# 32x32 transposes on VectorE in place of TensorE's turns of attention's output, and the first expert's mask made by ScalarE

## The reference

```python
# attention, no softmax over keys: the softmax runs over the 8 features of a head
scores = einsum('bhqk,bhsk->bhqs', qh, kh) / sqrt(8)
out = softmax(einsum('bhqs,bhsk->bhqk', scores, vh), axis=-1)
x = x + heads_side_by_side(out) @ wo_w.T + wo_b
# experts, on the normalised x (t), e = each of the two best experts
h1 = t @ w1.T + 2 * (t @ a1[e].T) @ b1[e].T
h3 = t @ w3.T + 2 * (t @ a3[e].T) @ b3[e].T
act = silu(h1) * h3
out_e = act @ w2.T + 2 * (act @ a2[e].T) @ b2[e].T
x = x + sum over e of weight[e] * out_e
```

## Time and profile before

| | |
|---|---|
| median of 3 runs | 298.84 us (298.49 to 299.08) |
| span of the profiled execution, first to last instruction | 296.7 us |
| time around the span (median less span) | 2.1 us |
| busy: PE, PEld, DVE, ACT, POOL | 287.4, 238.4, 221.4, 187.5, 187.0 us |
| mean granted TensorE clock | 0.992 |

### The profile page before, as it was taken

The page is one execution under the profiler, slowest core; times in us unless marked ns, Lnnn a source line. Parts: engine busy times, 40 slices in busy tenths (PEclk is TensorE's granted clock), DMA queues, the critical chain, the costliest instruction groups (busy, mean ns, idle before and its releaser), DMA issues. The chain is left out here.

```text
span 296.7 us, 4518 instructions
## 1 busy us (share of the span) xinstructions
PE 287.4 (97%) x1487; PEld 238.4 (80%) x1487; DVE 221.4 (75%) x607; ACT 187.5 (63%) x310; POOL 187.0 (63%) x186
## 2 busy tenths in 40 slices
PE   8779999999999999999999999999999999999995
PEld 6557888878888888888888888888888887878874
DVE  3878986995689658894589765895579965795295
ACT  1467967674945966757755868459656658655532
POOL 3375599288970889419990589608982389518930
PEclk9979999999999999999999999999999999999999
DMA  5720020200220021200211011200012000200002
GB/s 147 287 66 9 0 73 1 72 1 11 97 73 0 0 72 38 71 1 2 71 50 60 0 49 59 71 0 2 1 37 73 0 0 35 75 1 0 0 2 71
DMA packets 7225, 12.45 MB, mean 42 GB/s; under 512 B 1825, under 2 KB 3234, under 8 KB 7202
## 3 DMA queue, kind: packets, MB, share of 16 engines
q1 hardware_dynamic: 6768, 11.77, 12.0%
q10 hardware_dynamic: 434, 0.39, 0.4%
HBM read 10.03 MB, written 2.13 MB: 41 GB/s over the span
## 5 line engine op out<-in xcount | busy, mean ns | idle before, releaser
L989 ACT ACTIVATE silu<-h_ps 128x512 f32<-128x512 f32 x64 | 37.4, 596 | 31.4 <-PE h_ps L641 29.8
L1639 POOL TENSOR_TENSOR um_lo<-umf,um_hi 128x1024 fp32r<-128x1024 f32 x7 | 16.9, 2414 | 60.5 <-ACT um_hi L981 60.5
L641 PE MATMUL h_ps<-um_hi,b_hi 128*128 128x512 f32 x128 | 51.4, 401 | 0.0
L641 PE MATMUL h_ps<-um_lo,b_hi 128*128 128x512 f32 x128 | 50.3, 393 | 0.5 <-DVE um_lo L1309 0.5
L641 PE MATMUL h_ps<-um_hi,b_lo 128*128 128x512 f32 x128 | 49.9, 390 | 0.0
L1322 DVE TENSOR_TENSOR act_first<-silu,h_ps 128x512 f32<-128x512 f32 x32 | 21.4, 680 | 20.9 <-ACT silu L989 16.1
L1322 DVE TENSOR_TENSOR act_second<-silu,h_ps 128x512 f32<-128x512 f32 x32 | 21.7, 679 | 16.6 <-PE h_ps L641 14.7
L1661 POOL TENSOR_TENSOR scaled<-act_second,ratio 128x512 f32<-128x512 f32 x24 | 31.5, 1313 | 1.3 <-DVE act_second L1322 1.3
L641 PEld LDWEIGHTS h_ps<-um_lo,b_hi 128*128 128x128 f32 x128 | 24.0, 188 | 6.9 <-DVE um_lo L1309 1.4
L981 ACT CAST um_hi<-umf 128x1024 fp32r<-128x1024 f32 x14 | 14.8, 1055 | 23.2 <-DVE umf L1303 22.2
L641 PEld LDWEIGHTS h_ps<-um_hi,b_lo 128*128 128x128 f32 x128 | 24.1, 188 | 4.5
(11 more groups left out here) (278 smaller groups left out, 789.2 us busy)
## 6 DMA issues: line engine op xcount, KB each, us to landing
chosen<-choice_dram SPq DMA_DIRECT2D x7, 512.0 KB, 3.6
x_in<-in_x_dram SPq DMA_DIRECT2D x7, 256.0 KB, 2.9
ctx_in<-in_ctx_t_dram SPq DMA_DIRECT2D x7, 256.0 KB, 3.2
out_dram<-y SPq DMA_DIRECT2D x7, 256.0 KB, 2.0
act_second<-in_hidden_w_dram SPq DMA_DIRECT2D x1, 512.0 KB, 4.1
act_second<-in_lora_w_dram SPq DMA_DIRECT2D x1, 512.0 KB, 5.6
v_parts<-in_down_w_dram SPq DMA_DIRECT2D x1, 512.0 KB, 5.3
ctx_in<-in_ctx_t_dram ACTq DMA_DIRECT2D x2, 128.0 KB, 3.2
```

What stands on the lines that cost most here:

```text
L641: mm = nc.tensor.matmul((h1_ps, h3_ps)[s][n % 2][:], b13[w][:, s, c * P:(c + 1) * P], um[k][m][:, s, :], start=False, stop=(i == 2), skip_ ...
L989: nc.scalar.activation(silu[:, n % SILU_RING, :], h1_ps[n % 2][:], ACT.Silu).then_inc(silu_done.sem, 1)
L1639: nc.gpsimd.tensor_tensor(um[1][1][:], umf[1][:], as_f32(um[1][0][:]), ALU.subtract)\
```

## The change

From the third block on (`n >= AHEAD`, AHEAD = 2) the attention product gets its operands in reverse, so that `b_ps` holds features x tokens. `turn_o` on VectorE transposes each 32x32 square of it in place into `heads` (SBUF): a partition then holds tokens of one 32-group, and its columns the features of one group of four heads, so the softmax's groups of 8 lie side by side in the columns as before. Maximum and shift read `heads`. After GpSimd's division a second 32x32 transpose on VectorE, `turn_heads`, writes `heads_t`, which the projection reads; TensorE's turn and ScalarE's copy of it go for these blocks. The bank `b_ps` is free for the down products after `turn_o`.

For every block but the first the first expert's mask is made by ScalarE: |row's expert - chosen expert| (Abs) into `distance`, then Relu(1 - distance). It stands behind `z_high(b, 2)`, ahead of `ctx_high`, which `z_high(b, 2)` has passed. VectorE makes the second mask after `mask_u(0)`.

```diff
             def attention_out(n, i=WHOLE):
...
-                by_tile(o_bank(n, i), lambda t: q_t[:, t * P:(t + 1) * P], lambda t: ktv[:, t, :], i=i)\
-                    .then_inc(o_mm.sem, 1)
+                queries, pairs = (lambda t: q_t[:, t * P:(t + 1) * P]), (lambda t: ktv[:, t, :])
+                if n < AHEAD:
+                    by_tile(o_bank(n, i), queries, pairs, i=i).then_inc(o_mm.sem, 1)
+                else:
+                    by_tile(o_bank(n, i), pairs, queries, i=i).then_inc(o_mm.sem, 1)
...
             def project(n, i=WHOLE):
...
+                elif n >= AHEAD:
+                    pe.wait_ge(logits_done.sem, logits_done.of(n - 1))
...
-                        used = (ktv_done, o_shifted)[k]
-                        pe.wait_ge(used.sem, used.of(b + 2))
+                        if k == 0:
+                            pe.wait_ge(ktv_done.sem, ktv_done.of(b + 2))
+                        else:
+                            pe.wait_ge(o_turned, b + 3 - AHEAD)
...
                 hidden(b, 0)
                 hidden(b, 1)
-                turn_heads(b + 1)
...
+            def first_mask(n):
+                if n == 1:
+                    sc.wait_ge(row_expert_in, 16)
+                sc.wait_ge(chosen_in.sem, chosen_in.of(n))
+                nc.scalar.activation(tile4(distance), chosen_index(0), ACT.Abs, bias=row_expert_sb[:, 0:1], scale=-1.0)\
+                    .then_inc(expert_gap.sem, 1)
+                sc.wait_ge(expert_gap.sem, expert_gap.of(n))
+                if n > 1:
+                    sc.wait_ge(v_part_done.sem, v_part_done.of(n - 2))
+                    sc.wait_ge(umf_done.sem, umf_done.of(n - 2))
+                nc.scalar.activation(masks[n % 2][:, 0, :], distance[:], ACT.Relu, bias=1.0, scale=-1.0)\
+                    .then_inc(first_mask_done.sem, 1)
...
             exp_o(2)
             exp_ratio(1)
+            first_mask(1)
             ctx_high(3)
...
-                heads_turned(b + 1)
...
                 z_high(b, 1)
+                z_high(b, 2)
+                first_mask(b + 1)
                 if b + 3 < BLOCKS:
                     ctx_high(b + 3)
-                z_high(b, 2)
                 um_high(b + 1, 0)
...
+            def turn_o(n):
+                ve.wait_ge(o_mm.sem, o_mm.of(n))
...
+                nc.vector.transpose(flat(heads), o_bank(n, WHOLE)[:]).then_inc(o_turned, 1)
+
+            def turn_heads(n):
+                ve.wait_ge(heads_done.sem, heads_done.of(n))
+                ve.wait_ge(wo_mm.sem, wo_mm.of(n - 1))
+                nc.vector.transpose(heads_t[:], flat(heads)).then_inc(heads_t_done.sem, 1)
...
             mask_ktv(2)
-            act_step(0, 7)
+            turn_o(2)
             top_of_o(2)
             shift_o(2)
+            act_step(0, 7)
...
-            mask(1, 0)
             z_low(0, 1)
-            mask(1, 1)
             z_low(0, 2)
             mask_u(1, 0)
+            second_mask(1)
             mask_u(1, 1)
...
                 early = b + 2 < BLOCKS
+                turn_heads(b + 1)
                 act_step(b, 0)
...
                 if early:
+                    turn_o(b + 2)
                     top_of_o(b + 2)
                     shift_o(b + 2)
                 act_step(b, 7)
...
                 z_low(b, 1)
-                mask(b + 1, 0)
                 z_low(b, 2)
-                mask(b + 1, 1)
                 mask_u(b + 1, 0)
+                second_mask(b + 1)
                 mask_u(b + 1, 1)
```

More of the change, by code:

```diff
@@ L179, in build_program @@
         masks = [sb(f"masks{i}", [P, TOP, BLK]) for i in range(2)]
+        distance = sb("distance", [P, BLK])
         umf = [sb(f"umf{k}", [P, 2, BLK]) for k in range(TOP)]
@@ L290, in build_program @@
         top_o_done = signal("top_o_done", first=2)
+        o_turned = sem("o_turned")
+        expert_gap = signal("expert_gap", first=0)
+        first_mask_done = signal("first_mask_done", first=0)
         o_shifted = signal("o_shifted", first=2)
@@ L326, in build_program @@
         masks_mm = signal("masks_mm", TOP)
-        masks_done = signal("masks_done", TOP)
+        masks_done = signal("masks_done", 1, first=TOP)
         ratio_mm = signal("ratio_mm")
@@ L547, in turn_heads @@
                     pe.wait_ge(umf_done.sem, umf_done.of(0))
-                elif n > 1:
-                    pe.wait_ge(logits_done.sem, logits_done.of(n - 1))
                 turn(heads_bank(n, i), lambda t: heads[:, t, :], i).then_inc(heads_t_mm.sem, 1)
@@ L1186, in mask_ktv, with scores @@
                     .then_inc(ktv_done.sem, 1)
-            def top_of_o(n, i=WHOLE):
-                ve.wait_ge(o_mm.sem, o_mm.of(n, upto(i)))
-                o = o_bank(n, i)[:].rearrange("p (g k) -> p g k", k=DK)[:, groups(i)]
+            def scores(n, i):
+                src = o_bank(n, i) if n < AHEAD else flat(heads)
+                return src[:].rearrange("p (g k) -> p g k", k=DK)[:, groups(i)]
+            def turn_o(n):
+                ve.wait_ge(o_mm.sem, o_mm.of(n))
+                if n == AHEAD:
+                    ve.wait_ge(heads_t_mm.sem, heads_t_mm.of(n - 1))
+                else:
+                    ve.wait_ge(heads_t_done.sem, heads_t_done.of(n - 1))
+                nc.vector.transpose(flat(heads), o_bank(n, WHOLE)[:]).then_inc(o_turned, 1)
[3 more added lines that the diff above has]
+                nc.vector.transpose(heads_t[:], flat(heads)).then_inc(heads_t_done.sem, 1)
+            def top_of_o(n, i=WHOLE):
+                if n < AHEAD:
+                    ve.wait_ge(o_mm.sem, o_mm.of(n, upto(i)))
+                else:
+                    ve.wait_ge(o_turned, n + 1 - AHEAD)
+                o = scores(n, i)
                 nc.vector.tensor_reduce(top_o[:, groups(i)], o, AX_X, ALU.max).then_inc(top_o_done.sem, 1)
@@ L1248, in choose, with second_mask @@
                 op.then_inc(top_i_done.sem, 1)
-            def mask(n, k):
+            def second_mask(n):
                 ve.wait_ge(chosen_in.sem, chosen_in.of(n))
[L1252 to L1261, removed]
+                ve.wait_ge(first_mask_done.sem, first_mask_done.of(n))
+                dst, first = tile4(masks[n % 2][:, 1, :]), tile4(masks[n % 2][:, 0, :])
+                nc.vector.scalar_tensor_tensor(out=dst, in0=chosen_index(1), scalar=row_expert_sb[:, 0:1], in1=first,
+                                               op0=ALU.is_equal, op1=ALU.subtract).then_inc(masks_done.sem, 1)
             def first_onehots(i):
@@ L1299, in mask_u @@
                     ve.wait_ge(um_diff_lo.sem, um_diff_lo.of(n - 1))
-                ve.wait_ge(masks_done.sem, masks_done.of(n, k + 1))
+                if k == 0:
+                    ve.wait_ge(first_mask_done.sem, first_mask_done.of(n))
+                else:
+                    ve.wait_ge(masks_done.sem, masks_done.of(n))
                 for s in range(2):
```

## The result

The changed kernel takes 311.71 us (median of four runs, 310.92 to 312.43) and the kernel before 298.68 us in the same session: a ratio of 1.0438, 95% interval 1.0423 to 1.0453, so 13.0 us slower where 8.6 were forecast. The profiled span is 309.7 us. The time lies above the stated range of 302 to 311 us: direction and the chain of waits are as predicted, the size is not.

A forecast was written before the change was run, and what follows sets the result against it. TensorE was taken as the bound, with VectorE's chain to um_low level with it. Later um_low adds some 11.1 us, less TensorE's 2.5: 8.6 us on 298.84 gives 307.4 us, range 302 to 311.

The forecast's parts named there:

- turn_heads fits into VectorE's idle time: Before the first act_step: turn_heads hidden in VectorE's 2.48 us idle time; without that cover act_step is 0.7 us late.
- The second mask moves into the path: VectorE's second mask, 1.11 us from start to start, comes behind mask_u(0) and ahead of um_low, delaying um_low.
- TensorE has next to no slack at um_low: End of VectorE's chain: um_low ends at 132.14, its product starts at 132.34, so lateness reaches TensorE in full.
- half-rate transposes: Rival: VectorE's turn_o takes 1.18 in place of 0.69 us, adding 3.0 us over six chains: 310.4; 8 in 100.
- table reloads: Rival: Abs or Relu on ScalarE needs another table, 1.28 us per load: 316 us or above; 5 in 100.
- a mask in time: Rival: ScalarE's first mask comes early enough for mask_u(0), so 2.5 us come off: 296.3; 12 in 100.
- the size of um_low's lateness: In main periods um_low is 1.32 us late: mask_u(0) 0.21 late plus the second mask's 1.11.
- By period: Sum of um_low delays over seven masks: 6.6 + 3.67 + 0.78, some 11.1 us, less TensorE's 2.5: 8.6 us.
- a clock below 1.00: Sign of being wrong: TensorE's granted clock falls below 1.00 after the new pauses, adding time; no size given.
- 0.90 us net: Main loop periods grow 0.9 us: um_low 1.32 late, less 0.43 saved on TensorE.
- The turns' term: TensorE's removed turns of heads, behind the second hidden step, save 0.43 us each; six at 0.42 are 2.5 us.
- the 2.56 us forecast: Second block: mask_u(0) starts at 62.57 in place of 60.01; with the second mask's 1.11, 3.67 us late.

## Why the prediction came out too low

**What held.** VectorE's transposes take 0.72 and 0.71 us (forecast 0.73 and a neighbour's length), Abs 1.29 and Relu 0.63 (1.23 and 0.63). turn_heads fits into VectorE's idle time. The second mask moves into the path, and TensorE has next to no slack at um_low. One reading behind that was wrong: the waits in the earlier trace rows, two of weight loads and two of products, belong to the same two products (63.68 and 265.95 us), so two of the seven um_low were waited for, the first and the last, and not four. The rivals of half-rate transposes, table reloads and a mask in time are out: ScalarE loads tables 16 times in both kernels. That agrees with the Trainium skill (ScalarE: Activation LUTs, Table sets: the hidden batching unit), by which relu and abs lie in every set; the run with the mask moved up shows it for the place where SiLU's table is loaded as well.

**The term that was missing: the clock.** Two steps failed, this one and the size of um_low's lateness below. The sum under "By period" priced the second block's late um_low as waiting time alone. The stop also took TensorE to 0.50, which costs 2.7 us more by the trace. The text named a clock below 1.00 as something that would add to the time, but gave it no chance and no price, though its own sum had a stop of nearly 4 us in it.

**The terms that were too small.** In steady periods 0.90 us net was forecast (1.32 less 0.42); the starts of um_low are 34.2 to 34.3 us apart before and 35.4 to 35.6 after, so 1.15 to 1.33. TensorE's product behind um_low, beside the one at 132.34 in the earlier trace rows:

```profile
140.64 0.50 PE L648 MATMUL h_ps<-um_lo,b_hi 128*128 128x512 f32 x1 [1.20 <-DVE um_lo L1348]
```

Laid side by side, TensorE's timelines of the period give 1.35 us at um_low, 0.10 for the restart behind it and 0.11 at b_lo, less 0.43 for the turns: 1.13, and the rest in steps of some 0.03. The turns' term was right. um_low's was not: it ends 1.67 us later (13.30 against 11.63), not 1.32. The mask is 0.15 later than worked out, and from the first masked product to um_low it is 3.70 in place of 3.50 us, since the second product now waits for the mask just ahead of it (1.30 a step, not 1.11). Of the 1.67 some 0.15 was slack, which the forecast took as none (from um_low's end to its product 0.20 us before, 0.05 after), so some 1.5 us reach TensorE. The wait at b_lo, which was not seen at all, is a part of these and no cost on top: turn_o delays every VectorE result behind it, and what TensorE waits at b_lo it waits less at um_low. In the second block the first masked product is late by the 2.56 us forecast (turn_o to umf 9.87, where the reduction to umf was 7.30), but the rest of the chain by 1.63 in place of 1.11.

Put together: 4.18 in place of 3.67 us for the second block (from block 0's um_low to its own 35.17 us, before 30.99), 2.67 for the clock, 6.27 in place of 4.5 for five periods and 0.69 in place of 0.36 for the last make 13.8. The profiled executions differ by 13.0; the other 0.86 is how much later the profiled execution of before reached block 0's um_low (31.41 against 30.55), a start that lies anywhere from 30.3 to 32.1 in the kernels run here.

**What the forecast did not ask.** It took the queue position of the mask as given. The run with the gap's load behind z_high shows that this position, and not ScalarE's speed, makes most of the loss in the later blocks, though a shorter Abs would have made it smaller too (0.57 us a block). And it counted TensorE's 0.42 us per block as gained; the transposes alone lost 0.85%, as b_lo, um_low and the keys behind ctx_low were each as tight as TensorE, and only with all but b_lo loosened does some 0.3% remain.

## What to carry to other kernels

Work moved to an idle engine starts when that engine's queue lets it: look at what stands ahead of it and what that waits for, before its length. Moved to the front, it holds up what stands behind it while its own input has not landed, as in the last block here. When every end of a period is tight, a saving on the bound engine is worth only what the tightest of the other chains allows; list them all (here b_lo, z_low, um_low, ctx_low) before counting it. A forecast with a long new stop of TensorE in it needs a term for the clock behind the stop.

## What the hardware showed that was not expected

- TensorE's clock fell to 0.50 for some 6.6 us at stops of 1.03 and 2.13 us within 4 us, and for some 3.5 us at a single stop of 2.42 us; it did not fall at single stops of 1.2 us, one per period, and of 1.40 us.
- A VectorE mask with one tensor input, 0.72 us, took 1.77 beside a GpSimd pass that had begun 0.26 us earlier; the other way round GpSimd's 1.29 us pass took 2.04 beside a VectorE mask with two.
- A 32x32 transpose on VectorE of 128x512 fp32 takes 0.72 us from PSUM and 0.71 from SBUF, no more than its neighbours; Abs on a strided read of chosen took 1.29 us, on contiguous columns 0.72.
